# Splitting fp32 activations into three bfloat16 parts instead of two float32r parts in a binary-weight MLP

## The reference, cut to what matters

```python
    def _L3_ffn_ref(x, k0, k1, k2, s0, s1, s2):
        D_IN = 256
        FEATURES = (1024, 1024, 256)

        def _conn_dense(kernel_bool, x):
            w = jnp.where(kernel_bool, jnp.float32(1.0), jnp.float32(-1.0))
            return x @ w
        h = jnp.concatenate([x, -x], axis=-1)
        h = s0 * _conn_dense(k0, h)
        h = jax.nn.relu(h) * 2
        h = s1 * _conn_dense(k1, h)
        h = jax.nn.relu(h) * 2
        h = s2 * _conn_dense(k2, h)
        return h
    ...
    x = x + _L3_ffn_ref(_layernorm(x, axis=-1), L3_ffn_k0, ...)
```

## Time and profile before

| | |
|---|---|
| median of 3 runs | 2729.97 us (2723.89 to 2732.99) |
| profiled execution | 2729.97 us, its span 2728.2 us |
| TensorE busy | 2553.7 us (94%), mean granted clock 0.976 of full speed |
| VectorE busy | 1457.5 us (53%) |
| ScalarE busy | 995.9 us (37%) |
| GpSimd busy | 625.5 us (23%) |
| first matmul of the first product | 2635.52 us after the span's start |
| last matmul of the third product | ends at 2725.29 us |

### The profile page before, as it was taken

One profiled execution on the slowest core, in us unless ns is written; L12 is line 12 of the kernel. 1 busy time (PEld: TensorE's weight loads), 2 busy tenths in 40 slices (PEclk: granted clock), 3 DMA queues, 4 the chain that ended last, 5 costly groups with the idle time before them and its releaser, 6 DMA issues. The chain is left out here.

```text
span 2728.2 us, 47270 instructions
## 1 busy us (share of the span) xinstructions
PE 2553.7 (94%) x18498; PEld 1966.1 (72%) x18498; DVE 1457.5 (53%) x2397; ACT 995.9 (37%) x2147; POOL 625.5 (23%) x649
## 2 busy tenths in 40 slices
PE   8889996999999898979999997989999999989989
PEld 4566994666666656957888886976888886477768
DVE  4474224777777733035555556235555555389981
ACT  2252224666666421332222221213222222477731
POOL 2002002010100001013333330221333331057833
PEclk9999998999999998989999998999999999999999
DMA  9443873111110103942121112653221211022210
GB/s 286 136 139 111 300 271 97 47 33 33 48 32 17 51 1 122 330 151 74 59 70 59 59 36 103 225 172 100 71 66 51 70 59 41 1 70 86 82 39 16
DMA packets 97803, 260.04 MB, mean 95 GB/s; under 512 B 19028, under 2 KB 45368, under 8 KB 90184
## 3 DMA queue, kind: packets, MB, share of 16 engines
q1 hardware_dynamic: 86520, 240.17, 26.8%
q0 software_dynamic: 3840, 10.49, 1.2%
q10 hardware_dynamic: 7248, 6.65, 0.7%
HBM read 236.13 MB, written 21.14 MB: 94 GB/s over the span
## 5 line engine op out<-in xcount | busy, mean ns | idle before, releaser
L2192 POOL TENSOR_TENSOR buf<-buf 128x512 f32<-128x512 f32 x128 | 159.8, 1269 | 504.9 <-ACT buf L2326 504.9
L2351 DVE TENSOR_REDUCE buf<-acc 128x256 f32<-128x1024 f32 x128 | 150.8, 1220 | 218.9 <-PE acc L2219 218.9
L2252 PE MATMUL acc<-buf 128*128 128x256 f32 x1024 | 257.2, 384 | 3.6 <-ACT buf L2335 3.6
L2213 PE MATMUL acc<-buf 128*128 128x256 f32 x1024 | 236.6, 384 | 3.5 <-PEq L89 2.6
L2320 ACT COPY buf<-acc 128x256 f32<-128x256 f32 x64 | 23.8, 372 | 533.3 <-PE acc L2234 533.3
L2213 PEld LDWEIGHTS acc<-buf 128*128 128x128 f32 x1024 | 189.4, 190 | 36.9 <-issue 12.1
L2252 PEld LDWEIGHTS acc<-buf 128*128 128x128 f32 x1024 | 180.8, 190 | 37.5 <-issue 15.9
L2720 ACT ACTIVATE buf<-acc,buf 128x512 f32<-128x512 f32 x256 | 172.6, 686 | 75.1 <-DVE buf L2754 75.0
L2754 DVE TENSOR_REDUCE buf<-acc 128x1 f32<-128x512 f32 x256 | 159.0, 684 | 63.4 <-PE acc L2632 63.4
L2364 DVE TENSOR_TENSOR buf<-acc,buf 128x1024 f32<-128x1024 f32 x128 | 150.8, 1220 | 67.8 <-ACT buf L2320 67.8
L2644 PEld LDWEIGHTS acc<-identity,buf 128*128 128x128 f32 x1024 | 115.0, 141 | 84.0 <-issue 78.2
(11 more groups left out here) (420 smaller groups left out, 4812.1 us busy)
## 6 DMA issues: line engine op xcount, KB each, us to landing
buf<-in_L_ffn_W SPq DMA_DIRECT2D x52, 1024.0 KB, 6.9
buf<-in_ctx SPq DMA_DIRECT2D x48, 768.0 KB, 4.4
buf<-in_ctxT SPq DMA_DIRECT2D x64, 512.0 KB, 3.9
buf<-in_L_ffn_w SPq DMA_DIRECT2D x36, 704.0 KB, 5.8
buf<-state_rows SPq DMA_DIRECT2D x32, 512.0 KB, 3.6
buf<-in_ctxT SPq DMA_DIRECT2D x96, 128.0 KB, 4.1
buf<-in_L_ffn_w SPq DMA_DIRECT2D x18, 640.0 KB, 6.5
buf<-in_ctxT SPq DMA_DIRECT2D x32, 256.0 KB, 5.2
```

The source lines that it names most:

```text
L2192: pool.tensor_tensor(quarters[:, 2 * n:2 * n + 2, :], t[:, 4 * n:4 * n + 2, :], t[:, 4 * n + 2:4 * n + 4, :], ALU.add).then_inc(adding, 1)
L2213: pe.matmul(acc_s[:, n, :], ct0[x][:, tile(key_tile(n))], q0[:, b, 4 * y:4 * y + 4, :], start=(n % 2 == 0), stop=False)
L2252: pe.matmul(acc_m[:, 0:ROWS], ctx[x][:, key_tile(n), 0:P], probsT[y][:, n, :], start=(n == 0), stop=(n == KT - 1))
L2351: dve.tensor_reduce(most_of[n][:, :], acc_s[:, 4 * n:4 * n + 4, :].rearrange("p k r -> p r k"), AX.X, ALU.max).then_inc(part_most, 1)
```

## The change

Each fp32 activation becomes three bfloat16 parts in place of two float32r parts, and the weights are stored as bfloat16. The first part is not made by an instruction: it is a view of the upper 16 bits of each fp32 element, so that it is read with a step of two 2-byte elements. `rest = whole - first` is fp32 and made by DVE for every chunk; its upper 16 bits are the second part. `last = rest - second` is bfloat16 and made by POOL for every chunk. Each product is made three times. `whole` is a full buffer for each chunk, not four slots, so ACT no longer waits for a slot. For the first product, the turned features are copied to `xn_features` as fp32, and DVE makes `x_rest` and `x_last` from there, in two instructions of 1024 columns for each half.

```diff
+def upper_half(t):
+    return t.bitcast(BF16).rearrange("p m (n two) -> p m n two", two=2)[:, :, :, 1]
...
-        W0, W1, W2 = sb(P, DC, F, dtype=F32R), sb(P, FC, F, dtype=F32R), sb(P, FC, D, dtype=F32R)
-        upper, lower = [sb(P, FC, HALF, dtype=F32R) for _ in range(3)], [sb(P, FC, HALF, dtype=F32R) for _ in range(3)]
-        whole = xnT[:, :, :].rearrange("p k (h t) -> p (k h) t", h=2)
-        WHOLE = 2 * DC
+        W0, W1, W2 = sb(P, DC, F, dtype=BF16), sb(P, FC, F, dtype=BF16), sb(P, FC, D, dtype=BF16)
+        whole, rest = [sb(P, FC, HALF) for _ in range(3)], [sb(P, FC, HALF) for _ in range(3)]
+        last = [sb(P, FC, HALF, dtype=BF16) for _ in range(3)]
...
+        x_parts = (upper_half(xnT[:, :, :]), upper_half(x_rest), x_last)
+        parts = [(upper_half(whole[n][:, :, :]), upper_half(rest[n][:, :, :]), last[n][:, :, :]) for n in range(3)]
...
                     if g == 1:
-                        pe.wait_ge(x_split, 2 * DC)
-                    for n, x in enumerate((x_upper, x_lower)):
+                        pe.wait_ge(dve_copied, 2)
+                        pe.wait_ge(act_copied, 2)
+                    for n, x in enumerate(x_parts):
                         if n and g % 2 == 0:
-                            pe.wait_ge(x_split, DC * h + DC)
+                            pe.wait_ge((x_rested, x_lasted)[n - 1], h + 1)
...
                         if c % FC == 0:
-                            wait_split(pe, h * FC + k)
-                        for n, x in enumerate((upper[h], lower[h])):
+                            pe.wait_ge(lasted, h * FC + k + 1)
+                        for n, x in enumerate(parts[h]):
...
                         if j % 4 == 0:
-                            wait_split(pe, c)
-                        for n, x in enumerate((upper[home(c)[0]], lower[home(c)[0]])):
+                            pe.wait_ge(lasted, c + 1)
+                        for n, x in enumerate(parts[home(c)[0]]):
...
+                for h in range(2):
+                    dve.wait_ge(act_copied, h + 1)
+                    dve.wait_ge(dve_copied, h + 1)
+                    dve.tensor_tensor(x_rest[:, :, halves(h)], xnT[:, :, halves(h)], x_parts[0][:, :, halves(h)], ALU.subtract
+                                      ).then_inc(x_rested, 1)
+                    dve.wait_ge(x_rested, h + 1)
+                    dve.tensor_tensor(x_last[:, :, halves(h)], x_rest[:, :, halves(h)], x_parts[1][:, :, halves(h)],
+                                      ALU.subtract).then_inc(x_lasted, 1)
                 for c in range(2 * CHUNKS):
                     n, m = home(c)
                     dve.wait_ge(evicted, c + 1)
-                    dve.tensor_copy(upper[n][:, m, :], whole[:, c % WHOLE, :]).then_inc(rounded, 1)
-                    if by_dve(c):
-                        dve.wait_ge(rounded, c + 1)
-                        dve.tensor_tensor(lower[n][:, m, :], whole[:, c % WHOLE, :], upper[n][:, m, :].bitcast(F32),
-                                          ALU.subtract).then_inc(split_by_dve, 1)
+                    dve.tensor_tensor(rest[n][:, m, :], whole[n][:, m, :], parts[n][0][:, m, :], ALU.subtract
+                                      ).then_inc(rested, 1)
...
                     act.wait_ge(filled, c + 1)
-                    if c >= WHOLE:
-                        wait_split(act, c - WHOLE)
-                    act.activation(whole[:, c % WHOLE, :], chunk_bank(c)[:, :], ACT.Relu, scale=sc[:, c // CHUNKS:c // CHUNKS + 1]
+                    act.activation(whole[n][:, m, :], chunk_bank(c)[:, :], ACT.Relu, scale=sc[:, c // CHUNKS:c // CHUNKS + 1]
...
                 for c in range(2 * CHUNKS):
-                    if by_dve(c):
-                        continue
                     n, m = home(c)
-                    pool.wait_ge(rounded, c + 1)
-                    pool.tensor_tensor(lower[n][:, m, :], whole[:, c % WHOLE, :], upper[n][:, m, :].bitcast(F32), ALU.subtract
-                                       ).then_inc(split_by_pool, 1)
+                    pool.wait_ge(rested, c + 1)
+                    pool.tensor_tensor(last[n][:, m, :], rest[n][:, m, :], parts[n][1][:, m, :], ALU.subtract
+                                       ).then_inc(lasted, 1)
...
-        def split_features(dve, h, turned, dve_copied, act_copied):
-            dve.wait_ge(dve_copied, h + 1)
-            for c in (1, 0):
-                if c == 0:
-                    dve.wait_ge(act_copied, h + 1)
-                dve.tensor_tensor(x_lower[:, c, halves(h)], turned[c][h][:, :], x_upper[:, c, halves(h)].bitcast(F32), ALU.subtract
-                                  ).then_inc(work["x_split"], 1)
-        normed_jobs(chip, X, xn, x_upper, ident, [],
+        normed_jobs(chip, X, xn, xnT, ident, [],
```

More of the change, by code:

```diff
@@ L5 @@
 F32 = mybir.dt.float32
-F32R = mybir.dt.float32r
+BF16 = mybir.dt.bfloat16
 U8 = mybir.dt.uint8
@@ L187, in normed_jobs @@
 def normed_jobs(chip, src, keep, dst, ident, jobs, loads=(), gain=None, twice=False, sets=(), setup=None, early=None,
-                at=None, then=None, nbanks=4, also=None, stats=None, own=None, each_half=None):
+                at=None, then=None, nbanks=4, also=None, stats=None, own=None):
     nc = chip.nc
@@ L242, in _ @@
                                       ).then_inc(dve_copied, 1)
-                if each_half is not None:
-                    each_half(dve, h, turned, dve_copied, act_copied)
             if setup is not None:
@@ L651, in binary_mlp @@
         sb = buffers(chip, es)
-        W0, W1, W2 = sb(P, DC, F, dtype=F32R), sb(P, FC, F, dtype=F32R), sb(P, FC, D, dtype=F32R)
-        upper, lower = [sb(P, FC, HALF, dtype=F32R) for _ in range(3)], [sb(P, FC, HALF, dtype=F32R) for _ in range(3)]
-        whole = xnT[:, :, :].rearrange("p k (h t) -> p (k h) t", h=2)
-        WHOLE = 2 * DC
+        W0, W1, W2 = sb(P, DC, F, dtype=BF16), sb(P, FC, F, dtype=BF16), sb(P, FC, D, dtype=BF16)
+        whole, rest = [sb(P, FC, HALF) for _ in range(3)], [sb(P, FC, HALF) for _ in range(3)]
+        last = [sb(P, FC, HALF, dtype=BF16) for _ in range(3)]
         sc = sb(P, 3)
         k0, k1, k2 = (b.bitcast(U8) for b in front)
-        x_upper, x_lower = (t[2][:, 0:2 * DC, :].rearrange("p (k h) t -> p k (h t)", k=DC) for t in (upper, lower))
+        x_rest = whole[2][:, 0:2 * DC, :].rearrange("p (k h) t -> p k (h t)", k=DC)
+        x_last = last[2][:, 0:2 * DC, :].rearrange("p (k h) t -> p k (h t)", k=DC)
+        x_parts = (upper_half(xnT[:, :, :]), upper_half(x_rest), x_last)
+        parts = [(upper_half(whole[n][:, :, :]), upper_half(rest[n][:, :, :]), last[n][:, :, :]) for n in range(3)]
         def home(c):
@@ L664, in mlp @@
         def mlp(st, turned, banks, dve_copied, act_copied, act_steps, statistics):
-            (first_bits, scaled, x_split, filled, evicted, rounded, split_by_dve, split_by_pool, bits_by_act, bits_by_dve,
-             finished, stored) = st.sems(12)
+            (first_bits, scaled, x_rested, x_lasted, filled, evicted, rested, lasted, bits_by_act, bits_by_dve, finished,
+             stored) = st.sems(12)
             ring = banks + [turned[c][h] for c in range(DC) for h in range(2)]
[L668 to L675, removed]
+            work["bits"] = first_bits
             def chunk_bank(c):
@@ L696, in on_pe @@
                                 ins = pe.matmul(chunk_bank(c)[:, :], W0[:, k, tile(c % FC)], x[:, k, halves(h)],
-                                                start=(n == 0 and k == 0), stop=(n == 1 and k == DC - 1))
-                            if n == 1:
+                                                start=(n == 0 and k == 0), stop=(n == 2 and k == DC - 1))
+                            if n == 2:
                                 ins.then_inc(filled, 1)
@@ L706, in on_pe @@
                         if c % FC == 0:
-                            wait_split(pe, h * FC + k)
-                        for n, x in enumerate((upper[h], lower[h])):
+                            pe.wait_ge(lasted, h * FC + k + 1)
+                        for n, x in enumerate(parts[h]):
                             ins = pe.matmul(chunk_bank(c)[:, :], W1[:, k, tile(c % FC)], x[:, k, :],
-                                            start=(k == 0 and n == 0), stop=(k == FC - 1 and n == 1))
+                                            start=(k == 0 and n == 0), stop=(k == FC - 1 and n == 2))
                     ins.then_inc(filled, 1)
@@ L782, in early_bits @@
             dve.tensor_tensor(W0[:, :, :], k0[:, 0:2, :], k0[:, 2:4, :], ALU.subtract).then_inc(work["bits"], 1)
-        def split_features(dve, h, turned, dve_copied, act_copied):
-            dve.wait_ge(dve_copied, h + 1)
-            for c in (1, 0):
-                if c == 0:
-                    dve.wait_ge(act_copied, h + 1)
-                dve.tensor_tensor(x_lower[:, c, halves(h)], turned[c][h][:, :], x_upper[:, c, halves(h)].bitcast(F32), ALU.subtract
```

(5 more changed lines are left out.)

## The result

The changed kernel takes 2770.16 us (median of 4 runs, 2760.06 to 2774.41) against 2727.12 us before. The ratio is 1.0145, with a 95% interval from 1.0121 to 1.0169: on 2729.97 us that is +39.6 us, between 33 and 46. The forecast was +39.5 us, 2769.5 us.

The account below looks back on a forecast made before the run. TensorE was taken to bound the last layer: 480 matmuls at 220.0 ns plus 192 at 113.3 make 127.4 us against 87.9, +39.5 us. On 2729.97 us that gave 2769.5 us, range 2760 to 2779.

Parts of the forecast that it names:

- PE sets the layer's end, and a third pass has no cover: Last layer: its three products run end on end on TensorE, so the added matmuls lengthen it by 39.5 us.
- The distance of a bfloat16 matmul: All three products: start to start 220.0 ns for 512 columns, 113.3 for 256, between 213.3 to 226.7 and 106.7 to 120.0.
- The step of the argument that put one overhead on all of them: All three products: 512- and 256-column matmuls alike carry 13.4 ns beside their columns in float32r; bfloat16 was put midway.
- The slow clock stays: Start of the first product: the same gap ahead of PE leaves the 1.2 GHz stretch, 1.9 us counted on both sides.
- The first split is hidden: First product: DVE makes `x_rest` and `x_last` before PE wants them, so no lateness; about 2 us of cover left.
- The two subtractions are hidden: Chunks behind the first product: DVE then POOL in series, 2.0 us each, ready 2.2 us before PE wants the eighth.
- The 2.38 us that I kept for the upper end: Slower chunk cycle from the earlier timeline; it would make the eighth chunk's parts 0.8 us late, costed only at the upper end.
- The room at chunk 16: Start of the second product: the eighth chunk's parts ready at 2660.9, wanted at 2663.1, 2.2 us to spare.
- Signs: Expected profile: 96, 384, 192 records, 213 to 227 and 107 to 120 ns, first matmul near 2635.5, POOL subtractions 1.3 to 1.7 us.
- The starved GpSimd: Chunk 16: DVE takes the shared turn ahead of POOL, PE waits 4 us, perhaps 1.9 more; +45 us, 2775.4 us, chance 8%.
- The stepped operand: First two parts, read as every second 2-byte element, take two clocks a column: 459 ns, +116 us, 2846 us, chance 4%.
- Overlapping matmuls: All products: bfloat16 matmuls overlap, 113 and 60 ns, 65.8 us in total, 22 us faster, 2708 us, chance 4%.

Follow-up runs that it names:

- the packed experiment: Changed kernel with the second and third product using the packed bfloat16 part three times, the first two parts made but not multiplied; layer 130.28 us against 134.07.
- idle matmuls: Two-part float16 version of the kernel before, with four extra 256-column matmuls on TensorE ahead of the first product; ratios to before 0.9981 and 0.9979.

## Why the prediction was right, point by point

- *PE sets the layer's end, and a third pass has no cover.* Right. The chain holds PE alone, two parts cost 93.26 us and three 134.07, and moving the last subtraction to VectorE changes nothing.
- *The distance of a bfloat16 matmul, taken as the middle, 220.0 and 113.3 ns.* The sum of 127.4 us came out at 127.6 (480 x 0.2222 + 192 x 0.1092), and that is luck in part, because two misses cancel: the 512-column ones are 2.2 ns longer (+1.1 us) and the 256-column ones 4.1 ns shorter (-0.8 us). The step of the argument that put one overhead on all of them was wrong. A packed 16-bit operand costs its columns and 2.5 ns (215.8, 109.2), as the Trainium skill says (TensorE: Matmul & The Clock Gate, "Wait — 56ns, not 53.3ns?"), and the trace agrees for the packed operand alone. A stepped one costs 225.8 and 113.4. Two stepped and one packed make (2 x 225.8 + 215.8) / 3 = 222.5, against 222.2 measured. In the third product only the stationary operand is stepped, and that cost nothing: 109.2 ns with it and, in the packed experiment, without.
- *The slow clock stays.* Right here, and in seven more of these runs without idle matmuls. That it follows from the gap alone is not shown: in the packed experiment it did not come, with the same gap, the same first product and the same work ahead of it.
- *The first split is hidden.* Right, but with 0.3 us of cover and not 1.3. `x_rest` came 2.0 us after the first matmul, close to the 2.2 reckoned; the first eight matmuls took 2.3 us and not 3.5. That was a wrong reading of the earlier trace rows, where the clock is 0.98 until 2637.0, 1.5 us after the first matmul: only the last two or three of the eight run slow, in the trace before as in the one after. With the fast clock throughout (the packed experiment) a small wait appears here.
- *The two subtractions are hidden.* Right, and mis-sized: I reckoned 2.0 us a chunk in series. With 0.69 us more for each W1 block that made 18.8 us from the first eviction to the eighth split. The trace has 14.1 us (VectorE's first subtraction starts at 2647.0, the eighth split ends at 2661.1), and 1.44 us a chunk where no W1 block comes between (eight subtractions in 11.54 us). GpSimd's subtraction takes 1.04 us at the least, not 1.31: one input and the output are 2-byte elements now, and no run separates the two. Nor does it shut VectorE out for all of its time: in series the two would take 1.04 + 0.69 = 1.73. The 2.38 us that I kept for the upper end hold two casts as well, which the change drops. The room at chunk 16 was 6.9 us, not 2.2.
- *Signs.* The distances, the count of records, the chain without a wait and the slow clock came as listed. Two signs did not: the first matmul came at 2640.36 and not 2635.5, by the 4.8 us ahead of this layer, and the GpSimd subtractions took 1.04 to 1.49 us, not 1.3 to 1.7.
- *Rivals.* The starved GpSimd did not come in the changed kernel; made on purpose, with every subtraction doubled, it showed the wait and the slow clock behind it that the rival named: 2.7 and some 2 us, priced at 4 and 1.9. The stepped operand is slower, by 5% and not by the factor of two of that rival. Overlapping matmuls did not show: the 131 ns for 512 columns of the Trainium skill (TensorE: Matmul & The Clock Gate, "Back-to-back issue gap") stands against 215.8 ns measured, in a stream of loads and matmuls, and the measurement decides.

## What to carry to other kernels

Where TensorE is full, count passes first: a third pass cost 41 to 44 us here in either data type, and the cheaper type gave back 4.3. A free view of a wider number saves an instruction on an engine that may have time to spare and charges TensorE, which has none. By the measured 10.0 ns the stepped views of the changed kernel cost 320 x 10.0 ns = 3.2 us, an estimate; a kernel that packs them with instructions of their own was not run. Where there is a choice, store what is streamed packed, and let the stationary operand be the stepped one. When one layer changes, measure it from a landmark of its own; the whole time's scatter hid 1.7 us that the layer showed to the hundredth.

## What the runs showed of the hardware that I had not expected

- A float32r matmul costs 13.4 ns beside its columns at 256 and 512 alike, a packed bfloat16 or float16 one 2.5 ns at both, and a bfloat16 moving operand with a step of two elements 12.5 ns at 512 and 6.7 ns at 256. At these two sizes float32r's extra is the same for each matmul, and the step's grows with the columns. What makes float32r's was not tried; its longer weight loads (188 ns a record in the second product, against 96 for bfloat16) are one candidate.
- The same gap of 2.2 us ahead of a burst of matmuls was followed, 0.8 to 1.4 us into the burst, by 3.4 us at a granted clock of 0.50 (1.2 GHz) in nine of ten traces, and by no slow stretch in the tenth, whose code up to there was the same as in others of the nine.
- VectorE and GpSimd, each subtracting from memory to memory, slow each other to 1.44 us a chunk, and neither the sum of their times alone (1.73) nor the longer of them (1.04) gives that.
